# Order of VectorE's low parts and quarter sums in the first unit of a stage

## What is computed

```
x1 = attention part of the block (layer norm, three mixes, Wk, Wv, Wr, Wo)
h  = layer_norm(x1);  kk = mix(h) @ Wkey.T          # 512 -> 2048
x2 = x1 + sigmoid(mix(h) @ Wcr.T) * (silu(kk) @ Wval.T)
x  = x + x2
h  = layer_norm(x)
gate, up = split(h @ w_gate_up.T)                   # 512 -> 2 x 2048
out = x + (silu(gate) * up) @ w_down.T
```

## Time and profile before

| | us |
|---|---|
| median of 3 runs (lowest to highest) | 1066.68 (1066.46 to 1066.78) |
| the profiled execution's own time | 1066.69 |
| its span, first to last instruction | 1064.9 |
| TensorE busy | 1055.8 |
| VectorE busy | 634.6 |
| ScalarE busy | 483.8 |
| GpSimd busy | 541.7 |

### The profile page before, as it was taken

One profiled execution on the slowest core, in us unless ns is written; L12 is line 12 of the kernel. 1 busy time (PEld: TensorE's weight loads), 2 busy tenths in 40 slices (PEclk: granted clock), 3 DMA queues, 4 the chain that ended last, 5 costly groups with the idle time before them and its releaser, 6 DMA issues.

```text
span 1064.9 us, 13187 instructions
## 1 busy us (share of the span) xinstructions
PE 1055.8 (99%) x4748; PEld 874.7 (82%) x4748; DVE 634.6 (60%) x1104; ACT 483.8 (45%) x810; POOL 541.7 (51%) x453
## 2 busy tenths in 40 slices
PE   8999999999999999999999999999999999999998
PEld 7888888788888888888887888888888888888887
DVE  7887757785545565555468667676658333333334
ACT  7867566866444454333354433434354222222221
POOL 7776283635755545445355665655553333333321
PEclk9999999999999999999999999999999999999999
DMA  8002052277553345742413757563555464434422
GB/s 319 1 1 41 1 137 60 81 230 283 210 195 109 129 158 166 220 129 89 158 51 103 253 197 247 205 194 146 198 179 164 160 218 158 122 126 158 149 79 80
DMA packets 45234, 157.19 MB, mean 148 GB/s; under 512 B 4080, under 2 KB 4208, under 8 KB 40560
## 3 DMA queue, kind: packets, MB, share of 16 engines
q1 hardware_dynamic: 29712, 108.02, 29.2%
q0 software_dynamic: 15168, 48.24, 15.1%
q10 hardware_dynamic: 288, 0.09, 0.0%
HBM read 97.60 MB, written 58.72 MB: 147 GB/s over the span
## 4 chain that ended last, share of the span: by engine, by line
PE 87%; DVE 4%; POOL 4%; ACT 2%; DMA 1%; issue 1%; SPq 0%; DVEq 0%; ACTq 0%
PE bank L491 15%; PE bank L493 15%; PE bank L492 15%; PE bank L502 13%; PE bank L504 13%; PE bank L503 13%; POOL operand L1484 2%; DVE combo L1259 1%; DMA quart<-wide 1%; POOL weights L1472 1%; PE bank L664 1%; ACT made L757 1%; PE bank L566 1%; DVE resid L1285 1%; POOL weights L1484 0%
## 5 line engine op out<-in xcount | busy, mean ns | idle before, releaser
L1285 DVE TENSOR_TENSOR resid<-bank,resid 128x512 f32<-128x512 f32 x240 | 164.7, 689 | 232.8 <-PE bank L493 231.6
L1528 POOL TENSOR_TENSOR inner<-made,inner 128x512 fp32r<-128x512 f32 x128 | 166.6, 1323 | 194.3 <-ACT inner L884 194.3
L502 PE MATMUL bank<-combo,left 128*128 128x512 f32 x672 | 262.6, 391 | 1.3 <-POOL left L1506 1.0
L504 PE MATMUL bank<-combo,left 128*128 128x512 f32 x672 | 261.7, 390 | 0.0
L503 PE MATMUL bank<-combo,left 128*128 128x512 f32 x672 | 261.7, 389 | 0.0
L491 PE MATMUL bank<-right,inner 128*128 128x512 f32 x512 | 199.4, 389 | 0.0
L493 PE MATMUL bank<-right,inner 128*128 128x512 f32 x512 | 199.4, 389 | 0.0
L492 PE MATMUL bank<-right,inner 128*128 128x512 f32 x512 | 199.4, 389 | 0.0
L1506 POOL TENSOR_TENSOR left<-quart,left 128x512 fp32r<-128x512 f32 x96 | 115.3, 1224 | 91.7 <-ACT left L849 44.1
L502 PEld LDWEIGHTS bank<-combo,left 128*128 128x128 f32 x672 | 126.2, 188 | 29.1 <-POOL left L1506 1.9
L504 PEld LDWEIGHTS bank<-combo,left 128*128 128x128 f32 x672 | 126.2, 188 | 26.2
(11 more groups left out here) (135 smaller groups left out, 1503.3 us busy)
## 6 DMA issues: line engine op xcount, KB each, us to landing
kept_left<-left SPq DMA_DIRECT2D x24, 1792.0 KB, 8.1
left<-kept_left POOLq DMA_DIRECT2D x24, 1024.0 KB, 7.0
left<-kept_left POOLq DMA_DIRECT2D x24, 768.0 KB, 5.1
tall_staged<-tall SPq DMA_DIRECT2D x64, 256.0 KB, 2.8
quart<-wide SPq DMA_DIRECT2D x24, 512.0 KB, 4.2
raw<-kept SPq DMA_DIRECT2D x32, 256.0 KB, 6.0
landed<-wts SPq DMA_DIRECT2D x20, 256.0 KB, 5.7
resid<-x POOLq DMA_DIRECT2D x4, 1024.0 KB, 9.6
```

What stands on the lines that cost most here:

```text
L502: pe.matmul(acc[:], hi, combo[:, c, k, 0, :], start=fresh and k == 0, stop=False, skip_group_check=True)
L504: mm = pe.matmul(acc[:], lo, combo[:, c, k, 0, :], start=False, stop=k == 1, skip_group_check=True)
L1285: dve.tensor_tensor(tile, A[s][:], tile, ALU.add).then_inc(added, 1)
L1528: pool.tensor_tensor(inner[:, h % 4, i, 1, :], made_at(n), inner[:, h % 4, i, 0, :].bitcast(F32), ALU.subtract).then_inc(inner_lo, 1)
```

## The change

In the first unit of stages 1, 2 and 3 (units 8, 16 and 32) VectorE makes the two low parts of B22 later: no longer directly behind those of T4, but behind `some(1)` and ahead of `sum_v`. In unit 16, the only one of the three whose next unit has fresh left operands, the four sums for unit 17 move from behind `sum_v` to directly behind `seed`, ahead of the low parts of T4. GpSimd in unit 16 waits for the low parts up to T4 (40 of the count), no longer for those of B22 too (42).

```diff
                 if after is not None:
                     make_t2(after, range(1, 2))
                     combo_lo_of(after, T3)
+                if u + 1 in FRESH and u:
+                    sums(u + 1)
                 if stage_start(u) and u:
                     combo_lo_of(stage_of(u), T4)
-                    combo_lo_of(stage_of(u), B22)
-                if u + 1 in FRESH and not stage_start(u):
-                    sums(u + 1)
                 if is_key(u):
                     last_norm(u, 0)
                 some(1)
+                if stage_start(u) and u:
+                    combo_lo_of(stage_of(u), B22)
                 sum_v(u)
                 if u == 0:
                     first_chunk_right_lo()
-                if stage_start(u) and u and u + 1 in FRESH:
-                    sums(u + 1)
...
                 if u + 1 in FRESH:
                     if stage_start(u) and u:
-                        pool.wait_ge(combo_lo, 2 * SEVEN * (stage_of(u) + 1))
+                        pool.wait_ge(combo_lo, 2 * (SEVEN * stage_of(u) + made_place(stage_of(u), T4) + 1))
                     unit_left_lo(u + 1, 0)
```

## The result

| | before | after |
|---|---|---|
| median, us | 1066.67 (1066.29 to 1067.03, 22 runs) | 1068.97 (1067.28 to 1069.50, 22 runs) |
| profiled execution, own time, us | 1066.69 | 1067.63 |
| its span, us | 1064.9 | 1065.8 |
| mean granted clock of its TensorE | 1.000 | 1.000 |

The ratio over all runs is 1.0017 (95% interval 1.001 to 1.0024), that of the two medians 1.0022: slower, by a small amount that is clear of no change. The median lies 0.3 us above my range (1066.4 to 1068.7) and 1.3 us above my number; the ratio over all runs would put the time at 1068.5, just inside the range. The 22 runs of the changed kernel do not lie around their median. They make two groups: ten at mean granted clock 1.000 with a median of 1067.68 (1067.28 to 1068.07), and twelve at 0.998 with a median of 1069.13 (1068.96 to 1069.50). No run lies between 1068.07 and 1068.96.

The account below looks back on a forecast made before the run. TensorE, busy for 99% of the span, was taken as the bound, so only its gaps count: +2.23 - 1.23 = +1.00 us on 1066.69 gave 1067.7. The range was 1066.4 to 1068.7.

Parts of the forecast that it names:

- Parts 1 to 3: Unit 16: sums behind the seed end at 576.13, not 580.40; T4 makes TensorE about 0.03 us late; GpSimd starts 577.41.
- Part 4: Unit 16: B22's low parts are held beside GpSimd, sum_v ends at 581.00, new gap ahead of S4 x B22 2.23 us.
- the rival of unheld parts: Unit 16: B22's low parts are not held by GpSimd, gap 0.96 us, net -0.27, 1066.4; chance 0.14.
- a full turn for each part: Unit 16: B22's low parts both cost 1.71 to 1.74 us, gap 3.2, net +1.9, 1068.6; chance 0.13.
- GpSimd keeping the way: Unit 16: GpSimd empties its queue before B22's low parts run, gap 5.1 us, net +3.9, 1070.6; chance 0.10.
- Part 5: Unit 17: left low parts are ready before S3 x T3 is due, so its whole gap of 1.23 us is saved.
- Part 6: Units 8 and 32: B22's later low parts cost TensorE 0, at most 0.2 us in unit 32.
- Sum: Whole kernel: net +1.00 us from unit 16 on 1066.69 gives 1067.69, so 1067.7, forecast as no change.

Follow-up runs that it names:

- the 3.9 us gap: Changed kernel plus one more unused instruction like a low part of B22 in unit 16, ahead of sum_v: 1071.06 us, ratio 1.0043.

## Why the prediction was right and where it failed

**Parts 1 to 3 (sums, T4, GpSimd's release).** Right. The sums start 0.60 behind the seed and take 1.46 us; ScalarE's copy starts at 576.12 (I had 576.17), GpSimd at 577.36 (577.41); the whole trace stands 0.05 us earlier there, by its seed. TensorE was not late at A22 x T4.

**Part 4 (B22 beside GpSimd).** Right in mechanism and size. The turns between VectorE and GpSimd give 2.53 us for two low parts where I had 2.55 (577.85 to 580.40), and a gap of 2.21 where I had 2.23. The experiment that only gives GpSimd its old wait brings the parts back to 1.29, so this is shown and not only argued. Its gap of 0.93 is also what the rival of unheld parts had put at 0.96: the price was right and the condition was not there. That rival falls with it, and so do those of a full turn for each part and of GpSimd keeping the way.

**Part 5 (the old gap).** Right: no gap at S3 of unit 17. GpSimd's held instruction took 1.71 us (I had 1.74), and its last one ends at 582.72 (582.8).

**Part 6 (units 8 and 32).** Right: no gap, and alone they make 0.16 us, within the spread. `sum_v` in unit 32 had 0.28 us to spare where I had 0.1 to 0.2.

**Sum.** Here it failed. The net of +1.00 holds for the runs at clock 1.000: 1067.68 against 1067.7. The step that failed is the one from the gap to the time. I priced the new gap on TensorE by its length alone, because the one before had cost its length at granted clock 1.00, and I had read no row that would test a gap nearly twice as long. In 20 of the 34 runs of the changed kernel the mean clock was 0.998 and the time about 1.45 us longer; the trace of one of them shows some 3.4 us at the 1.2 GHz level behind the gap. The median therefore lies in the second group, at +2.3 us. A second term of 0 or about 1.5 us behind the first was missing, and the range would have had to reach 1069.5 to hold both. That something over half of the runs have the second term, and so carry the median with them, could not be read from the kernel before. That the ratio over all runs still falls inside the range is luck: it averages a group that the sum gives with one that it lacks.

The prediction also took 0.2%, 2.1 us, as about what a measurement can tell, and called its +1.0 us no change on that ground. The interval above is 0.07% to either side: the measured 0.17% lies under that line and is still clear of no change.

The runs bound the cause from both sides. With gaps of 0.8 to 1.5 us ahead of S4 x B22 none of 44 runs has 0.998, and none of the 81 runs of the kernel before measured with them, whose gap of 1.23 stands ahead of S3; with 2.2 us it is 26 of 45 in two kernels, one with GpSimd beside VectorE and one without; with 3.9 us it is 5 of 5. That a gap of this length in this place brings the lower clock is shown by these. What gaps between 1.5 and 2.2 us do, and whether the wait of 0.28 us ahead of S1 x T1, which stands in all of these kernels, has a part in it, was not measured. Why one run of the same kernel falls and another doesn't is not shown by any trace here. The Trainium skill, "TensorE: Matmul & The Clock Gate", Part 1, says that the activity behind the gate is measured by a timer which runs free of the kernel, so that the point of a change varies from run to run. Two groups of one kernel, and a fall directly behind the gap in one trace but 1.3 us later in that of the 3.9 us gap, agree with it; they do not prove it.

## What to carry to other kernels

An engine's wait that looks needless can keep it silent at the right moment. Before letting GpSimd go earlier, list what VectorE does then with two SBUF sources, and who waits for that. In a chain that is late, first push back the work that nobody waits for (here two output tiles) rather than the work whose deadline is the next one. A gap on TensorE need not cost only its length: here it did up to 1.5 us, and at 2.2 us it did in 19 of 45 runs. Read the single runs and their granted clocks, since a median between two groups describes neither.

## What the runs showed of the hardware

- VectorE instructions with two SBUF sources take turns with GpSimd's: two took 2.53 us beside GpSimd and 1.29 when it was silent, with a third beside it 1.75 against 0.69. GpSimd's 512-column instruction took 1.71 instead of 1.30, so each of the two engines delays the other. Instructions with a source in a bank kept 0.68 to 0.69.
- A gap of 2.2 us on TensorE was followed by the lower clock level in 26 of 45 runs; gaps up to 1.5 us in none of 44. In a trace of it the lower level lasted about 3.4 us (581.10 to 584.53). It cost 1.6 us there, and 1.45 between the medians of the two groups.
- The fall may come later than the gap: at 3.9 us TensorE ran at full speed from 582.98 to 584.24 first.
